# Two heads' attention scores contracted over their own 50 rows, in two row groups of TensorE

## What is computed

```
qkv = x @ Wqkv + bqkv                                # 256 -> 768
att = softmax(causal(q @ k^T * 16 ** -0.5))          # per head, 512 x 512
x = layernorm(x + (att @ v) @ Wout + bout)
h = silu(x @ w1^T * s1) * (x @ w2^T * s2)            # 256 -> 1024
h = gelu(h @ h1^T * sh1); h = gelu(h @ h2^T * sh2)   # 1024 -> 1024, twice
out = layernorm(x + h @ w3^T * s3)                   # 1024 -> 256
```

## Time and profile before

| | |
|---|---|
| time of the runs | 2169.16 us median of 2 (2168.17 and 2170.16) |
| the profiled execution | span 2166.8 us from its first to its last instruction; what lies around it is not in the trace |
| TensorE | busy 2118.4 us (98% of the span), 16294 matmuls |
| weight loads | 1878.8 us (87%) |
| VectorE, ScalarE, GpSimd | 1259.9, 1316.1, 492.9 us (58%, 61%, 23%) |
| chain that ended last | 89% TensorE |

### The profile page before, as it was taken

How to read it: one execution, slowest core, us unless ns; L and a number is a source line. 1 busy time by engine, 2 the same in 40 slices (tenths; PEclk the granted TensorE clock), 3 DMA queues, 4 the chain that set the end, 5 groups by cost and what they waited for, 6 DMA issues and landing times.

```text
span 2166.8 us, 52048 instructions
## 1 busy us (share of the span) xinstructions
PE 2118.4 (98%) x16294; PEld 1878.8 (87%) x16294; DVE 1259.9 (58%) x3928; ACT 1316.1 (61%) x2807; POOL 492.9 (23%) x899
## 2 busy tenths in 40 slices
PE   8789999999999999999999999999999999999998
PEld 4368889989889888899989889988999898988998
DVE  7765555556555565556556565565556556565452
ACT  6456566666556666566666666666566666656553
POOL 2222122221222222122221122222122132122220
PEclk9889999999999999999999999999999999999999
DMA  8742332232322332332232322333232232321100
GB/s 275 239 120 63 77 71 70 61 81 64 90 65 61 82 74 69 75 69 73 61 81 64 90 64 62 81 76 73 71 76 70 56 82 69 83 64 37 37 6 10
DMA packets 95940, 167.69 MB, mean 77 GB/s; under 512 B 19204, under 2 KB 38404, under 8 KB 95672
## 3 DMA queue, kind: packets, MB, share of 16 engines
q1 hardware_dynamic: 91912, 152.75, 28.6%
q10 hardware_dynamic: 3760, 11.54, 1.5%
HBM read 98.26 MB, written 68.17 MB: 77 GB/s over the span
## 4 chain that ended last, share of the span: by engine, by line
PE 89%; DVE 1%; DMA 0%; issue 0%; SPq 0%; ACT 0%; POOL 0%; POOLq 0%; DVEq 0%
PE ring L1241 44%; PE ring L1226 10%; PE pM L1116 7%; PE pS L1104 6%; PE pO L1164 6%; PE ring L1254 5%; PE ring L1176 4%; PE ring L1206 2%; PE ring L1196 2%; PE ring L1148 1%; PE ring L1215 1%; DMA qk_d<-c 0%; SPq L614 0%; DVE full_g L960 0%; DMA Qs<-nm 0%
## 5 line engine op out<-in xcount | busy, mean ns | idle before, releaser
L921 DVE CUSTOM_DVE_ANT_0 pM<-pM,mask 128x512 f32<-128x512 f32 (+3 forms) x1024 | 498.7, 502 | 366.1 <-PE pM L1116 292.3
L1241 PE MATMUL ring<-Yhi,H 128*128 128x256 f32 x1984 | 501.7, 289 | 0.0
L1241 PE MATMUL ring<-Xhi,H 128*128 128x256 f32 x1984 | 497.9, 288 | 0.0
L1241 PE MATMUL ring<-Ylo,H 128*128 128x256 f32 x1984 | 489.2, 282 | 0.0
L1241 PE MATMUL ring<-Xlo,H 128*128 128x256 f32 x1984 | 486.4, 282 | 0.0
L1241 PEld LDWEIGHTS ring<-Ylo,H 128*128 128x128 f32 x1984 | 377.8, 190 | 7.2 <-issue 3.4
L1241 PEld LDWEIGHTS ring<-Yhi,H 128*128 128x128 f32 x1984 | 377.0, 190 | 7.1 <-issue 3.4
L1241 PEld LDWEIGHTS ring<-Xlo,H 128*128 128x128 f32 x1984 | 379.1, 191 | 0.8
L1241 PEld LDWEIGHTS ring<-Xhi,H 128*128 128x128 f32 x1984 | 378.4, 191 | 1.0 <-issue 0.2
L1116 PE MATMUL pM<-Ks,Qs 128*128 128x512 f32 x992 | 304.2, 340 | 20.6 <-DVE mx L921 9.0
L865 ACT ACTIVATE Yhi<-ring,cols 128x256 fp32r<-128x256 f32 x248 | 117.8, 475 | 266.8 <-PE ring L1241 170.1
(11 more groups left out here) (146 smaller groups left out, 3518.7 us busy)
## 6 DMA issues: line engine op xcount, KB each, us to landing
qk_d<-c SPq DMA_DIRECT2D x120, 256.0 KB, 3.4
Qs<-qk_d SPq DMA_DIRECT2D x120, 192.0 KB
Ks<-qk_d SPq DMA_DIRECT2D x120, 192.0 KB
qk_d<-c SPq DMA_DIRECT2D x120, 128.0 KB, 3.0
xTs<-in_xT SPq DMA_DIRECT2D x16, 512.0 KB, 4.3
raw<-in_h SPq DMA_DIRECT2D x8, 1024.0 KB, 10.4
xz<-in_x SPq DMA_DIRECT2D x16, 512.0 KB, 3.9
H<-raw ACTq DMA_DIRECT2D x8, 1024.0 KB, 9.3
```

Source lines behind the costliest of these rows:

```text
L921: nc.vector.tensor_tensor_reduce(pM[:, h % 2, 0:n], pM[:, h % 2, 0:n], mask[:, T - n:T], 1.0, NEG, ALU.add, ALU.max, mx[:, t, h:h + 1]).th ...
L1241: mm = nc.tensor.matmul(to, w, x_part, start=(k == 0 and m == 0), stop=(k == KB - 1 and m == 1))
```

## The change

The stack of Q loses the plane per head: `Qs` is [128, 2, 2, 512] like K, and holds both heads of a pair in rows 0 to 49 and 64 to 113. A matmul now contracts over the 50 rows of its head alone, and the two heads of a pair are issued one behind the other, into bank 0 and bank 1 of pM or pS. TensorE's instructions have tiles of 64 rows by 128 columns at row 0 and row 64, where they had 128 by 128.

A step is now a unit of two banks, 512 columns in each, five a group for max and for exp alike: units 0 and 1 are block 0 of pair 0 and 1 (512 columns), units 2 and 3 block 1 (384) and block 3 (128) of a pair, unit 4 block 2 (256) of both pairs. A unit is 2 or 4 matmuls. ScalarE does two exponentials of 512 columns a unit, VectorE one maximum for each block and head as before, GpSimd 7 masks a group instead of 8. Exp has 16 matmuls a group for 12, max 16 as before.

The lists are rewritten with the five units in place of the 16 and 11 steps, in the old order of the rest: a unit stands where the steps it replaces stood. probs_b is wider, a new probs_c takes block 2, the small buffers that lay over Xlo and Ylo go. The memsets of the four stacks go, and the first batch's copies of Q are one instruction instead of two.

```diff
-        Qs = sb("Qs", [P, 2, PAIRS, 2, T], F32R)
+        Qs = sb("Qs", [P, 2, PAIRS, T], F32R)
...
+        def blocks_of(e):
+            if e < 2:
+                return [(0, e, 0)]
+            if e < 4:
+                return [(1, e - 2, 0), (3, e - 2, T - P)]
+            return [(2, p, p * T // 2) for p in range(PAIRS)]
```

ScalarE's part of an exp unit:

```diff
-                        nc.scalar.activation(dst, src, ACT.Exp, scale=SCALE).then_inc(exp_done, 1)
+                        for s in range(2):
+                            nth = g * UNITS_G + 2 * e + s
+                            act.wait_ge(e_ready, b * UNITS + nth + 1)
+                            nc.scalar.activation(unit_probs(e)[:, s], pS[:, s], ACT.Exp, scale=SCALE).then_inc(exp_done, 1)
```

TensorE's part of an exp unit:

```diff
-                        need(pe, exp_done, b * UNITS + nth - 1)
-                        for p in sorted({p for p, _ in heads}):
-                            wide = [k for k, (m, _) in enumerate(heads) if m == p]
-                            first, last = heads[wide[0]][1], heads[wide[-1]][1]
-                            mm = nc.tensor.matmul(pS[:, nth % 2, n * wide[0]:n * (wide[-1] + 1)],
-                                                  K[:, p, kt * P:(kt + 1) * P],
-                                                  Q[:, p, first:last + 1, kt * P:T], start=True, stop=True)
-                        mm.then_inc(e_ready, 1)
+                        nth = b * UNITS + g * UNITS_G + 2 * e
+                        blocks = blocks_of(e)
+                        for m, (kt, p, at) in enumerate(blocks):
+                            n = e_cols(kt)
+                            for s in range(2):
+                                rows = slice(SROWS * s, SROWS * s + STACK)
+                                if m == 0:
+                                    need(pe, exp_done, nth + s - 1)
+                                mm = nc.tensor.matmul(pS[:, s, at:at + n], K[rows, p, kt * P:(kt + 1) * P],
+                                                      Q[rows, p, kt * P:T], start=True, stop=True)
+                                if m == len(blocks) - 1:
+                                    mm.then_inc(e_ready, 1)
```

TensorE's part of a max unit:

```diff
-                        need(pe, m_done, nth - 1)
-                        nc.tensor.matmul(pM[:, h % 2, 0:n], Q[:, h // 2, h % 2, t * P:(t + 1) * P],
-                                         K[:, h // 2, 0:n], start=True, stop=True).then_inc(m_ready, 1)
+                        for m, (kt, p, at) in enumerate(blocks):
+                            t, n = TB - 1 - kt, e_cols(kt)
+                            for s in range(2):
+                                rows = slice(SROWS * s, SROWS * s + STACK)
+                                if m == 0:
+                                    need(pe, m_done, nth + s - 1)
+                                mm = nc.tensor.matmul(pM[:, s, at:at + n], Q[rows, p, t * P:(t + 1) * P],
+                                                      K[rows, p, 0:n], start=True, stop=True)
+                                if m == len(blocks) - 1:
+                                    mm.then_inc(m_ready, 1)
```

The first line of ORDER:

```diff
-max:0:1:3:0 max:0:1:3:1 y:-1:0:0 table:0:Exp:0 exp:0:0:0 y:-1:0:1 max:0:1:3:2 max:0:1:3:3 exp:0:0:1 y:-1:1:0
+max:0:1:0 y:-1:0:0 table:0:Exp:0 y:-1:0:1 max:0:1:1 exp:0:0:0 y:-1:1:0 h2:-2:1:0:0 exp:0:0:1 h2:-2:1:0:1 exp:0:0:2
```

More of the change, by code:

```diff
@@ L72 @@
[L72 to L76, removed]
@@ L82 @@
[L82 to L86, removed]
@@ L127 @@
-weight_test:0:9 raw:0:10 v:1:3 max:1:1:2:3 exp:1:0:7 max:1:1:1:0 qk:1:2 exp:1:0:8 stack:1:2 y:0:0:0 y:0:0:1
-y:0:1:0 max:1:1:1:1 exp:1:0:9 exp:1:0:10 max:1:1:1:2 y:0:1:1 max:1:1:1:3 max:1:1:0:0 max:1:1:0:1 ln1_stats:0
-max:1:1:0:2 max:1:1:0:3 weights:0:10 pv:1:0:1 neg_split:1:1 weight_test:0:10 neg_max:1:1 ln1:0 low_bits:0 qk:1:3
-exp:1:1:0 exp:1:1:1 x1_turn:0:0 exp:1:1:2 x1_turn:0:1 max:1:2:3:0 exp:1:1:3 exp:1:1:4 o_out:1:0 weight_flag:0
+table:0:Exp:0 qk:0:0 raw:0:0 qk:0:1 stack:0:0 raw:0:1 columns:0 qk:0:2 max:0:0:0 stack:0:1 raw:0:2 max:0:0:1 v:0:0
@@ new lines @@
+max:0:0:2 qk:0:3 max:0:0:3 stack:0:2 max:0:0:4 stack:0:3 load_x:0 v:0:1 neg_split:0:0 weights:0:0 max:0:1:0
+weights:0:1 bias:0 neg_max:0:0 raw:0:3 max:0:1:1 raw:0:4 v:0:2 max:0:1:2 exp:0:0:0 max:0:1:3 v:0:3 exp:0:0:1 load_xT:1
+max:0:1:4 exp:0:0:2 weights:0:2 raw:0:5 neg_split:0:1 exp:0:0:3 weights:0:3 pv:0:0:0 max:0:2:0 exp:0:0:4 neg_max:0:1
+max:0:2:1 raw:0:6 pv:0:0:1 max:0:2:2 o_out:0:0 exp:0:1:0 raw:0:7 max:0:2:3 exp:0:1:1 max:0:2:4 weight_test:0:0
+weights:0:4 qk:1:0 exp:0:1:2 raw:0:8 pv:0:1:0 exp:0:1:3 exp:0:1:4 neg_split:0:2 max:0:3:0 neg_max:0:2 pv:0:1:1
@@ new lines @@
+exp:0:2:0 weights:0:5 o_out:0:1 max:0:3:1 exp:0:2:1 max:0:3:2 max:0:3:3 exp:0:2:2 max:0:3:4 exp:0:2:3 weight_test:0:1
+weights:0:6 pv:0:2:0 stack:1:0 raw:0:9 neg_split:0:3 weight_test:0:2 exp:0:2:4 neg_max:0:3 pv:0:2:1 weight_test:0:3
+weight_test:0:4 o_out:0:2 exp:0:3:0 qk:1:1 exp:0:3:1 max:1:0:0 exp:0:3:2 weights:0:7 pv:0:3:0 exp:0:3:3
+weight_test:0:5 max:1:0:1 weights:0:8 exp:0:3:4 max:1:0:2 o_out:0:3 weight_test:0:6 pv:0:3:1 max:1:0:3 v:1:0
+weight_test:0:7 max:1:0:4 weights:0:9 den:0 weight_test:0:8 stack:1:1 v:1:1 v:1:2 neg_split:1:0 rec_save:0 neg_max:1:0
@@ L131 @@
+max:1:1:0 exp:1:0:0 max:1:1:1 exp:1:0:1 max:1:1:2 exp:1:0:2 den_turn:0 rec_load:0 weight_test:0:9 raw:0:10 v:1:3
+max:1:1:3 exp:1:0:3 qk:1:2 stack:1:2 y:0:0:0 y:0:0:1 y:0:1:0 max:1:1:4 exp:1:0:4 y:0:1:1 ln1_stats:0 weights:0:10
+pv:1:0:1 neg_split:1:1 weight_test:0:10 neg_max:1:1 ln1:0 low_bits:0 qk:1:3 exp:1:1:0 x1_turn:0:0 x1_turn:0:1
+exp:1:1:1 o_out:1:0 weight_flag:0
 """
 FIRST_ORDER = """
-table:0:Exp:0 max:0:2:3:1 table:0:Gelu:1 table:0:Exp:2 max:0:2:3:2 gu:-1:0:0 gu:-1:0:1 exp:0:1:5 max:0:2:3:3
@@ L581, in move @@
                         Q, K = stacks(steps, off, g)
-                        first = steps is HEAD and off == 0
-                        if first and g < PICKED:
+                        if steps is HEAD and off == 0:
                             continue
@@ L1089, in iteration @@
                     if kind == "exp":
-                        g, u = a
-                        kt, heads = heads_of(u)
-                        n, nth = e_cols(kt), g * EXP_UNITS[-1] + u
+                        g, e = a
                         Q, K = stacks(steps, off, g)
-                        if u == 0:
+                        if e == 0:
                             pe.wait_ge(nm_in, (b * NG + g + 1) * 64)
-                        elif steps is HEAD and u == 2:
+                        elif steps is HEAD and e == 1:
```

320 lines of the change are left out of this document (126 added, 194 removed).

## The result

Two runs took 2221.14 and 2207.03 us, median 2214.09, beside 2169.16: a ratio of 1.021, 95% interval 1.013 to 1.029. The change makes the kernel some 2.1% slower. The forecast was 2200 us, slower by 1.4%.

What follows compares the result with a forecast made beforehand. TensorE was taken to bound each turn. Score products falling from 19.9 to 9.4, switches of 11.2 and waits of 1.5 gave +2.2 us a turn, +32 over 14.6 turns, first batch 0: 2200 us, range 2075 to 2265.

Steps and rivals of the forecast that it cites:

- The steady turn: One turn of the loop over batches: 129.5 - 19.9 + 9.4 + 11.2 + 1.5 = 131.7 us, +2.2.
- Side by side: Score products: the two heads of a pair run together at one head's pace, 9.4 us per turn, 10.5 less.
- Switches: TensorE's changes between full array, row tiles and column tiles: 56 more per turn at 0.20 us, 11.2 us.
- Waits: Score units waiting for ScalarE or VectorE to free their banks: 1.5 us per turn, bounds 0 and 4.
- (c): Score matmuls: tiling takes no effect in fp32r, pairs run one after the other without drains; +29, 2198 us; chance 0.10.
- gain of 1.75x: Score pairs: two row tiles might gain 1.75x instead of 2, making the sum 1.8 us a turn higher.
- the term for the first batch: First batch: memsets and copies go, 38 switches come, 57 units get shorter; 0, within 8 us either way.
- the counting of the second batch and the last as ordinary turns: Score units outside the first batch's list: counted as 583/40 = 14.6 turns at +2.2, +32 us.
- (a): Steady turn: row tiles side by side, but switches cost little; -4.5 a turn, 2103 us, faster; chance 0.25.
- (b): Score pairs: the two heads' weight loads go one after the other through one port; 2327 us; chance 0.15.
- my case: Whole kernel: pairs side by side, each switch 0.20 us; 2200 us, own range 2140 to 2255; chance 0.50.
- TensorE's busy time would fall, as drains show as idle: Steady turn: a sign for the prediction's own case, TensorE's busy time below its 129.50 us; no size of fall given.

Runs made afterwards that it cites:

- e2: Kernel after, but both heads of a pair use the same row tile (head 1 gets head 0's scores): 2346.69 us, 1.082 to before, turn 140.4.
- e1: Kernel after with every score matmul on the full array, rows 0 to 113 (sums of two heads): 2197.38 us, 1.013 to before, turn 131.5.
- e3: Kernel after with full-array score matmuls in the first batch's list alone: 2208.27 us, 1.017 to before, first y step at 116.3.
- e7: Kernel after with every score matmul over rows 0 to 64 (wrong scores for head 1): 2204.54 us, 1.016 to before, first y step at 122.8.
- e10: The kernel after itself, unaltered, run four times more beside seven runs of before: 2214.62 us, 1.021 to before, turn 132.0.
- e8: Kernel after with only the exp units on the full array, max units still in row tiles: 2227.35 us, 1.027 to before, turn 132.9.
- e4: Kernel after with only the order changed, max units right behind exp units of their number, 20 runs: 2234.32 us, 1.030 to before.
- e5: Kernel after with only the order changed, max units behind exp units or, where banks were held, beside pv, 24 runs: 2177.79 us, 1.0042 to before.

## Why the prediction was right, and where it was not

**The steady turn was right: 131.7 forecast, 132.0 measured**, and for the reasons that it gave.

- Side by side: 9.4 us for all pairs. A lone unit takes 0.43 us where e2's takes 0.66, and the 0.23 saved are half of its four 256-column matmuls; the sum had 0.24 for what is left. Row groups in fp32r do what the column tiles of the earlier trace rows did.
- Switches: 56 x 0.20 = 11.2. By a lone unit's starts it is 30 x (0.20 + 0.19) = 11.7, in the parts that were read from L1164: 0.09 for going in, 0.10 for leaving, and 0.10 for each of the two uncovered loads.
- Waits: 1.5 forecast, 1.3 left over in the sum of the runs. Some are units close behind one another, as described. One max unit of the turn:

```profile
1098.24 0.91 PE L1060 MATMUL pM<-Ks,Qs 50*128 50x256 f32 x4
1099.08 0.38 PE L1187 MATMUL ring<-Xhi,H 128*128 128x256 f32 x1
```

  Its four records last 0.91, where the lone unit's above last 0.50, and the next FFN start is 0.84 behind it instead of 0.43: head 1's first matmul comes 0.41 after head 0's instead of beside it.
- ScalarE's exponentials cost nothing of their own: it is busy 81.26 us a turn, for 81.36. e1 says what TensorE pays for 16 exp matmuls instead of 12 when nothing overlaps: 131.5 - 129.6 = 1.9 with waits, where rival (c) had 2.0.
- The closeness of the sum is in part luck. The score matmuls took 21.3 us by their starts before, and not 19.9, so 1.4 more went away than forecast. What came instead was 0.5 more for the switches, 0.9 more in the other full-array work (0.7 of it in e1 too) and 0.3 in pv, 1.7 in all.
- The prediction's estimate for a gain of 1.75x was off in its own sum: the pairs would then take 2 x 9.4 / 1.75 = 10.8 us, 1.4 more and not 1.8.

**The step that failed is the term for the first batch, "0, within 8 either way"**, and the counting of the second batch and the last as ordinary turns. Together they cost 23.4 us where the sum had 1.6 x 2.2 = 3.5. With this +20 the forecast of 2200 becomes 2220, 6 above the median (the profiled execution was the slower of the two runs). I had taken TensorE's matmuls there to be hidden by VectorE's waits and did not ask at which clock they ran. From 70 to 125 us its clock was at 0.75 and 0.77 even before the change. With 50 rows a matmul it is at the 1.2 GHz level for most of 40 to 125 us, and the first y step comes 8.5 us later: e3 gives 8.2 of them back, and e1 against e7 shows the rows as what matters. Of the interval that follows, e3 gives 2 of 5.5 us back (against e10's profile), or 5 of 8.7 (against the first). For the last interval, 6.2 us, the clock is 0.95 in one stretch of 35 us and 1.00 in the others. TensorE has a wait there that the kernel before does not have (who waited for whom, us, times, longest):

```profile
PE pM L1060 <- DVE mx L857: 1.9, 2, 1.5
```

By starts the score matmuls take 17.1 us in this interval for 18.7, so that they gain 1.6 us and not the 4.6 of a steady turn. e1 has 126.0 there, e3 131.1, e8 128.3. Why the maxima are late at this place stays open: nothing was run for it alone.

**The rivals.** (a), cheap switches, and 2103 us: out, by the late entries and by e2. (b), loads one after the other: out, the unit's four loads take 0.30 us, and two heads' matmuls start 3 ns apart. (c), no side by side: its 2198 is almost e1's 2197.38, which is that kernel; the median alone could not have told it from my case, the starts within a unit do. The mark "TensorE's busy time would fall, as drains show as idle" was wrong: it is busy 131.60 of 131.90 us. A record of 256 columns lasts 0.28 us where the next starts after 0.12, so it reaches over the 0.09 us by which a unit starts late. One has to look at starts. The other marks of being right came: 3 ns between the two heads' starts, 0.21 us from the last FFN start, no load ahead, 0.22 for the first FFN matmul behind, and 16.7 us a turn for the score matmuls, where 15 to 21 was named.

## What to carry to other kernels

A pair of row tiles saves half of the matmuls' time, 0.23 us for two of 512 columns, and each run of tiled matmuls among full ones costs 0.39 (some 0.3 by whole turns, where late units hide a part). So tiles pay when a run holds at least two such pairs (0.46 saved), and then hardly, and not for one alone. Before tiling, count the runs in the order that TensorE walks, not the matmuls; then look whether the engines that empty the banks can take units that stand so close (e4 lost 5.5 us a turn to that, e5 found the places where they can). And look at the granted clock of a stretch that TensorE does not seem to bound: where it is already under 1.00, matmuls over fewer rows can cost time, 8.2 us in the first batch here.
